# Delta-rule loop: products with keys, decays and head outputs move from GpSimd to VectorE, the squares of keys and queries to ScalarE

## The reference, cut to what matters

```python
q = q / (norm(q) + 1e-06);  k = k / (norm(k) + 1e-06)        # 8 heads of 64
...
def step(carry, ins):                                        # over the 64 tokens
    alpha = sigmoid(at + asp * spike)                        # decay of each channel
    beta  = sigmoid(bt[..., None] + sum(spike * bsp, -1, keepdims=True)) * active
    s = s * alpha[..., None]
    pred = einsum('bhk,bhkv->bhv', kt, s)
    s = s + (beta * kt)[..., None] * (vt - pred)[:, :, None, :]
    out = einsum('bhk,bhkv->bhv', qt, s)
...
y = y * rsqrt(mean(y * y, -1, keepdims=True) + EPS) * head_norm_w
y = x + y.reshape(B, T, H * dv) @ Wo * gate
z = _rms(y, ff_norm_w)
y = y + silu(z @ Wff1) * (z @ Wff3) @ Wff2
```

## Time and profile before

| what | value |
|---|---|
| three timed executions | 2277.12, 2288.8 and 2290.23 us, median 2288.8 |
| profiled execution, span of its instructions | 2277.7 us (its time as a whole is not listed apart from the span) |
| delta stage in it | about 887 to 1854 us of the span |
| busy over the span | PE 80%, DVE 65%, ACT 47%, POOL 32% |
| period of one group in the middle of the loop | 112.7 us: (1708.22 - 1032.03) / 6, from the starts of the first matmul L2341 of groups 1 and 7 |

### The profile page before, as it was taken

How to read it: one execution, slowest core, us unless ns; L and a number is a source line. 1 busy time by engine, 2 the same in 40 slices (tenths; PEclk the granted TensorE clock), 3 DMA queues, 4 the chain that set the end, 5 groups by cost and what they waited for, 6 DMA issues and landing times. The chain is left out here.

```text
span 2277.7 us, 76504 instructions
## 1 busy us (share of the span) xinstructions
PE 1818.4 (80%) x33033; PEld 1305.7 (57%) x33033; DVE 1481.3 (65%) x3245; ACT 1073.9 (47%) x2111; POOL 730.0 (32%) x824
## 2 busy tenths in 40 slices
PE   6999999998688453688989888988886778556774
PEld 4667766766566221365656565656565567544553
DVE  4777777776533776668676868686858343775544
ACT  3666566665233542555555555555554524312322
POOL 0111111111066501435353535353435110306773
PEclk9999999999589786799999999999999965557886
DMA  5000000000211111000000000000000030001114
GB/s 191 12 2 11 11 12 7 2 2 2 88 45 48 45 51 41 7 13 4 17 3 17 3 17 3 17 3 8 8 3 8 3 113 5 11 28 40 53 52 133
DMA packets 43091, 65.02 MB, mean 29 GB/s; under 512 B 6824, under 2 KB 27824, under 8 KB 41992
## 3 DMA queue, kind: packets, MB, share of 16 engines
q1 hardware_dynamic: 35720, 45.70, 6.1%
q0 software_dynamic: 7040, 14.43, 2.2%
HBM read 41.27 MB, written 18.84 MB: 26 GB/s over the span
## 5 line engine op out<-in xcount | busy, mean ns | idle before, releaser
L2800 POOL TENSOR_TENSOR delta_scaled_beta_k<-delta_scaled_beta_k,delta_decays 128x256 f32<-128x256 f32 x160 | 139.4, 893 | 274.3 <-PE bank L2353 274.3
L2920 DVE COPY_PREDICATED delta_neg_a_and_p_t<-delta_level_int,bank 128x512 f32<-128x512 uint8 x192 | 164.2, 923 | 33.5 <-PE bank L2353 24.8
L2353 PE MATMUL bank<-weights_sb,delta_scaled_beta_k 64*64 64x64 f32 x6144 | 121.1, 227 | 74.7 <-POOL delta_scaled_beta_k L2800 44.9
L721 POOL TENSOR_TENSOR attn_probs<-attn_probs,attn_row_sum 128x512 f32<-128x512 f32 x64 | 65.4, 1042 | 344.1 <-DVE attn_row_sum L809 344.1
L2353 PEld LDWEIGHTS bank<-weights_sb,delta_scaled_beta_k 64*64 64x64 f32 x6144 | 108.5, 141 | 96.9 <-issue 96.6
L2957 DVE STREAM_TRANSPOSE delta_inverse_t<-delta_inverse 64x512 f32<-64x512 f32 (+1 forms) x192 | 135.4, 705 | 21.9 <-ACT delta_inverse L2590 20.1
L300 PE MATMUL bank<-attn_z_self_t,weights_sb 128*128 128x256 f32 x512 | 126.4, 386 | 6.7 <-ACT attn_cross_keys L591 3.0
L2584 ACT ACTIVATE delta_two_less_ax<-bank 128x512 f32<-128x512 f32 x160 | 86.5, 597 | 88.0 <-PE bank L2374 86.7
L309 PE MATMUL bank<-attn_w_value_out,attn_z_self_t 128*64 128x512 f32 x512 | 124.3, 606 | 3.0 <-DVE x_all L768 2.7
L617 ACT ACTIVATE attn_probs_t<-bank 128x512 f32<-128x512 f32 x128 | 69.9, 595 | 116.1 <-PE bank L412 116.1
L2590 ACT ACTIVATE delta_inverse<-bank 128x512 f32<-128x512 f32 x128 | 69.3, 595 | 111.3 <-PE bank L2384 111.2
(11 more groups left out here) (545 smaller groups left out, 4665.9 us busy)
## 6 DMA issues: line engine op xcount, KB each, us to landing
weights_sb<-in_w_moe_dram SPq DMA_DIRECT2D x1, 4352.0 KB, 16.8
z_rows<-moe_z_all SPq DMA_DIRECT2D x16, 256.0 KB, 2.6
weights_sb<-moe_outs SPq DMA_DIRECT2D x8, 512.0 KB, 7.3
weights_sb<-in_w_delta_dram SPq DMA_DIRECT2D x1, 2816.0 KB, 11.7
weights_sb<-in_ctx_tok_dram SPq DMA_DIRECT2D x8, 264.0 KB, 4.9
attn_x_channels<-in_x_dram SPq DMA_DIRECT2D x8, 256.0 KB, 3.2
weights_sb<-in_w_self_dram SPq DMA_DIRECT2D x2, 1024.0 KB, 9.2
attn_ctx_channels<-in_ctxT_dram SPq DMA_DIRECT2D x8, 256.0 KB, 2.6
```

The source lines that it names most:

```text
L2353: last = pe.matmul(two[eo][rows(sg), u], kr[r, hp, t], second(kq[r, g % 2, :, hp, t], c), start=first, stop=True, skip_group_check=True)
L2800: pool.tensor_tensor(r_[:, :, 0, :], r_[:, :, 0, :], a_[:, :, 1, 0:1].to_broadcast([128, T // (2 * c), c]), ALU.mult)\
L2920: last = dve.copy_predicated(second(AP[:, eo, hps(P), :, :, :].rearrange("p h b i n -> p (h b i) n"), c), m_, two[eo][:, :].rearrange("p ( ...
```

## The change

Three kinds of products leave GpSimd for VectorE: `scale_k`, `scale_decay` and `o_normed`. On GpSimd the first two were one instruction for each head pair, on VectorE one instruction covers a half, two head pairs, so their counts halve (160 to 80 and 128 to 64); `o_normed` stays at 32. They are put into VectorE's order by hand behind the `scale` of their half, and the head outputs behind the decay products of levels 0 and 1.

The 64 squares of keys and queries leave GpSimd for ScalarE, which now reads bank J twice: first the square, then the copy that frees the bank. The squares of keys still go to `sqk`; those of queries go to the two spaces of `tmp` and the two of `orstd`, which the tail of the group two before uses. So before each square of a query ScalarE waits until the sums of that tail are done (`ss_ps`) and until all its head outputs are normalized (`o_normed`). GpSimd keeps the reset of the mask tile, the token normalization and the residual.

```diff
+
+def q_square(j):
+    return (tmp, orstd)[j // 2][:, j % 2, :]
...
-                last = pe.matmul(out_[r, 0:HALF], cnt_w[:, j, 0:32], sqk[:, j, HALF * half:HALF * half + HALF], start=j == 0,
+                x_ = q_square(j) if q else sqk[:, j, :]
+                last = pe.matmul(out_[r, 0:HALF], cnt_w[:, j, 0:32], x_[:, HALF * half:HALF * half + HALF], start=j == 0,
...
-            pe.wait_ge(s["scaled_kr"], 20 * g + HDP * (l - 1) + 2 * P + 2)
+            pe.wait_ge(s["scaled_kr"], 10 * g + 2 * (l - 1) + P + 1)
...
         for j in js:
             act.wait_ge(s[kind + "_ps"], nth_of(kind, g, j))
+            if kind == "k":
+                if g >= 1:
+                    act.wait_ge(s["nrm_part"], 8 * g)
+                    act.wait_ge(s["q_sum"], g)
+                if g >= 3:
+                    act.wait_ge(s["dn_ps"], g - 2)
+                square_ = sqk[:, j, :]
+            else:
+                if g >= 1:
+                    act.wait_ge(s["nrm_part"], 8 * g)
+                if g >= 2:
+                    act.wait_ge(s["ss_ps"], nth_of("ss", g - 2, 3))
+                    act.wait_ge(s["o_normed"], HDP * (g - 1))
+                square_ = q_square(j)
+            act.activation(square_, J[at_fill[kind, g, j] % 2][:, :], ACT.Square).then_inc(s["squared"], 1)
             act.activation(kq[:, g % 2, 0 if kind == "k" else 1, j, :], J[at_fill[kind, g, j] % 2][:, :], ACT.Copy)\
                 .then_inc(s[kind + "_rd"], 1)
 
...
-    def scale_k(g, l, P):
...
-        for hp in range(2 * P, 2 * P + 2):
...
-            pool.tensor_tensor(r_[:, :, 0, :], r_[:, :, 0, :], a_[:, :, 1, 0:1].to_broadcast([128, T // (2 * c), c]), ALU.mult)\
-                .then_inc(s["scaled_kr"], 1)
...
-    def scale_decay(g, l, P):
...
-    def squares(kind, g):
...
-    def o_normed(g, j):
...
-        if core:
-            scale_k(it, 0, 0)
-        if tail:
-            o_normed(it - 1, 0)
-        if core:
-            scale_k(it, 0, 1)
-        if tail:
-            o_normed(it - 1, 1)
-        if core:
-            scale_decay(it, 0, 0)
-            scale_decay(it, 0, 1)
...
+    def halves(t, c):
+        return t.rearrange("p h (m two c) -> p h m two c", two=2, c=c)
+
+    def scale_k(g, l, P):
+        c = 1 << l
+        dve.wait_ge(s["products"], 14 * g + 2 * (l + 1) + P + 1)
+        if l == 0:
+            dve.wait_ge(s["kr_rd"], nth_of("kr", g, 2 * P + 1))
+        else:
+            dve.wait_ge(s["scaled_kr"], 10 * g + 2 * (l - 1) + P + 1)
+            dve.wait_ge(s["scaled_decay"], 8 * g + 2 * (l - 1) + P + 1)
+        r_, a_ = halves(kr[:, hps(P), :], c), halves(al[:, g % 2, hps(P), :], c)
+        m = T // (2 * c)
+        if c == 1:
+            dve.tensor_tensor(r_[:, :, :, 0, 0], r_[:, :, :, 0, 0], a_[:, :, :, 1, 0], ALU.mult).then_inc(s["scaled_kr"], 1)
+        else:
+            dve.tensor_tensor(r_[:, :, :, 0, :], r_[:, :, :, 0, :], a_[:, :, :, 1, 0:1].to_broadcast([128, 2, m, c]), ALU.mult)\
+                .then_inc(s["scaled_kr"], 1)
+
+    def scale_decay(g, l, P):
+        a_ = halves(al[:, g % 2, hps(P), :], 1 << l)
+        dve.wait_ge(s["scaled_kq"], 24 * g + HDP * (l + 1) + 2 * P + 2)
+        dve.wait_ge(s["scaled_kr"], 10 * g + 2 * l + P + 1)
+        if l > 0:
+            dve.wait_ge(s["scaled_decay"], 8 * g + 2 * (l - 1) + P + 1)
+        dve.tensor_tensor(a_[:, :, :, 0, 0], a_[:, :, :, 0, 0], a_[:, :, :, 1, 0], ALU.mult).then_inc(s["scaled_decay"], 1)
+
+    def o_normed(g, j):
+        dve.wait_ge(s["o_rstd"], HDP * g + j + 1)
+        dve.tensor_tensor(oT[:, j, :], oT[:, j, :], orstd[:, j % 2, :], ALU.mult).then_inc(s["o_normed"], 1)
...
             masked(it, 1, 0)
             scale(it, 0, 0)
             scale(it, 0, 1)
+            scale_k(it, 0, 0)
             masked(it, 1, 1)
             scale(it, 0, 2)
             scale(it, 0, 3)
+            scale_k(it, 0, 1)
+            scale_decay(it, 0, 0)
+            scale_decay(it, 0, 1)
+        if tail:
+            o_normed(it - 1, 0)
+            o_normed(it - 1, 1)
+        if core:
             masked(it, 2, 0)
             scale(it, 1, 0)
             scale(it, 1, 1)
+            scale_k(it, 1, 0)
             masked(it, 2, 1)
             scale(it, 1, 2)
             scale(it, 1, 3)
+            scale_k(it, 1, 1)
+            scale_decay(it, 1, 0)
+            scale_decay(it, 1, 1)
+        if tail:
+            o_normed(it - 1, 2)
+            o_normed(it - 1, 3)
+        if core:
             first_turned(it, 0)
             first_turned(it, 1)
...
             scale(it, 2, 0)
             scale(it, 2, 1)
+            scale_k(it, 2, 0)
             turned(it, 1, 0)
             masked(it, 3, 1)
             scale(it, 2, 2)
             scale(it, 2, 3)
+            scale_k(it, 2, 1)
+            scale_decay(it, 2, 0)
+            scale_decay(it, 2, 1)
             turned(it, 1, 1)
         if front:
```

More of the change, by code:

```diff
@@ L2783, in _ @@
                 def _(pool):
-                    def halves(t, c):
-                        return t.rearrange("p (m two c) -> p m two c", two=2, c=c)
                     def reset(g):
@@ L2852, in _ @@
                         core, front, tail = 0 <= it < NG, 0 <= it + 1 < NG, it >= 1
-                        if core:
-                            scale_k(it, 0, 0)
-                        if tail:
-                            o_normed(it - 1, 0)
-                        if core:
-                            scale_k(it, 0, 1)
-                        if tail:
-                            o_normed(it - 1, 1)
-                        if core:
-                            scale_decay(it, 0, 0)
-                            scale_decay(it, 0, 1)
-                        if tail:
-                            o_normed(it - 1, 2)
-                            o_normed(it - 1, 3)
-                        if core:
-                            scale_k(it, 1, 0)
-                            scale_k(it, 1, 1)
-                            scale_decay(it, 1, 0)
-                            scale_decay(it, 1, 1)
-                        if front:
-                            squares("k", it + 1)
-                        if core:
-                            scale_k(it, 2, 0)
-                            scale_decay(it, 2, 0)
-                            scale_k(it, 2, 1)
-                            scale_decay(it, 2, 1)
-                        if front:
-                            squares("q", it + 1)
-                        if core:
-                            scale_k(it, 3, 0)
-                            scale_decay(it, 3, 0)
-                            scale_k(it, 3, 1)
-                            scale_decay(it, 3, 1)
                         if tail:
                             residual(it - 1)
-                        if core:
-                            scale_k(it, 4, 0)
-                            scale_k(it, 4, 1)
                         if front:
@@ L2935, in scale @@
                         if l > 0:
-                            dve.wait_ge(s["scaled_decay"], 16 * g + HDP * (l - 1) + hp + 1)
+                            dve.wait_ge(s["scaled_decay"], 8 * g + 2 * (l - 1) + hp // 2 + 1)
                         v = kq[:, g % 2, :, hp, :].rearrange("p i (m two c) -> p i m two c", two=2, c=c)[:, :, :, 1, :]
@@ L3103, in _ @@
                             scale(it, 3, 1)
+                            scale_k(it, 3, 0)
                         if front:
@@ L3112, in _ @@
                             scale(it, 3, 3)
+                            scale_k(it, 3, 1)
+                            scale_decay(it, 3, 0)
+                            scale_decay(it, 3, 1)
                             turned(it, 2, 0)
@@ L3120, in _ @@
                             scale(it, 4, 1)
+                            scale_k(it, 4, 0)
                             turned(it, 3, 0)
@@ L3124, in _ @@
                             scale(it, 4, 3)
+                            scale_k(it, 4, 1)
                             turned(it, 3, 1)
```

23 lines of the change are left out of this document (removed).

## The result

| | kernel before | changed kernel |
|---|---|---|
| median of four timed runs | 2288.7 us | 2323.4 us |
| lowest and highest | 2277.1, 2290.2 us | 2320.7, 2326.3 us |
| span of the profiled execution | 2277.7 us | 2324.4 us |

The ratio is 1.0175 [1.0148, 1.0201]: slower by 1.75%, 34.7 us between the medians. The forecast was 2320.

The account below looks back on a forecast made before the run. TensorE leads, with 44.9 us of waits for GpSimd, but VectorE is nearly full; 7.0 us lost less 2.2 gained in each of six groups is 28.8, with the edges +31 on 2288.8: 2320 us, range 2298 to 2340.

Parts of the forecast that it names:

- Steps 1 and 2: First half, group 4: ScalarE's key squares delay the second `first_inverse` to 1395.4; VectorE's last head output follows 6.3 us later.
- Step 3: First half: ScalarE's square of query 0 waits for the last head output, so `f_cb` starts 6.45 us later.
- Step 4: First half: TensorE's clock drops after the idle time; `f_cb` and `t_wo` take 8.4 us, `ax` loses 7.0.
- Second half: The wait before level 4 goes, VectorE is late next; gain 2.2 us per group, ends 0.7 and 4.2.
- about 1 us carried over from level 2: Second half, group 2: delay VectorE was to bring along ahead of its transposes at 1205.16.
- The relief: VectorE gets back about 7 us per group without GpSimd's disturbance, most in `scale`, which would take 0.69 us throughout.
- rival C: Faster: head outputs done before ScalarE asks, at 1395.4, so the new wait is empty; 36 us gained, 2253; chance 0.08.
- Edges: Outside groups 1 to 6: group 0 and stage start 0, group 7 about 3 us longer, last tail 0.7 shorter.
- A: Rival: clock recovers behind the gap and the second half gains more; 0.7 us lost per group, 2295; chance 0.27.
- B: Rival: VectorE limits the second half too, so nothing is gained there; 44 us slower, 2333; chance 0.12.

Follow-up runs that it names:

- run 3: Changed kernel with head outputs 2 and 3 moved ahead of the mask copy of level 1, half 1, in VectorE's queue: 0.9971 of the kernel before.
- run 6: Kernel before with only the squares of keys and queries moved to ScalarE, all products staying on GpSimd: 0.9964 of the kernel before.
- run 8: Kernel before with only key and decay products moved to VectorE, squares and head outputs staying on GpSimd: 1.0114 of the kernel before.
- run 7: Changed kernel with head outputs 2 and 3 ahead of the mask copy and key and decay products back on GpSimd: 0.9915 of the kernel before.
- run 4: Changed kernel with the four head outputs per group back on GpSimd: 0.9986 of the kernel before.
- run 2: Changed kernel with ScalarE copying queries 0 and 1 first and squaring them later from the copies, behind `f_cb`: 1.0093 of the kernel before.
- run 12: Run 7 with only the key squares late, made on ScalarE from the copies behind its part of `f_cb`: 0.9958 of the kernel before.

## Why the prediction was right

**Steps 1 and 2, right.** In group 4, in times of before, the second `first_inverse` ended at 1396.4 (1414.88 + 2.84 - 21.3), forecast 1395.4; ScalarE's queue cost 2.5 us and not 1.5. The last head output ended at 1402.9, forecast 1401.7: 6.5 us behind its releaser where the sum said 6.3.

**Step 3, right.** Six waits of 7.0 to 8.0 us, 45.4 in all. `f_cb` starts 6.3 us later in the mean (26.3 to 32.6), forecast 6.45. Run 3 shows the cause.

**Step 4, right in size.** From `f_cb` to `ax` 8.4 us in the mean, forecast 8.4; it was 7.6. The loss of the first half is 7.2, forecast 7.0. The granted clock of the first half of group 4 was 0.81 where it had been 0.95. But from `f_cb` to `ax` it is only 0.9 us of the loss: before, five of the six `f_cb` (groups 1 to 5) already ran mostly at the low level behind 3.5 us, their first 16 records taking 3.4 to 3.7 us and not 1.95.

**Second half, right, with two terms mis-sized.** Gain 1.8 (78.8 to 77.0), forecast 2.2. The wait before level 4 went, as forecast, since the queries' squares no longer stand ahead of the key product, and VectorE was late next. Counted from `ax`, as means over groups 1 to 6, the products of level 4 start 2.8 us earlier (27.6 to 24.8), the first `xw` behind the wait 1.5 (29.0 to 27.5; in group 2 it waits 2.19 us for VectorE's transposes), the second 2.6 (33.9 to 31.3; forecast 2.1 for group 2). Two terms are off:

- "about 1 us carried over from level 2" did not come. In group 2 the first transposes behind the wait started 0.5 us earlier and not later (1222.67 less 17.97, the distance of the two `ax`, is 1204.70, before 1205.16), and the second ended at 1209.8, forecast 1210.8. The terms as written also give ends 0.5 us later than the 1207.8 and 1210.8 that the sum goes by.
- What comes behind that second `xw` was left out of the sum for groups 1 to 6. From there to the group's end the gain falls from 2.6 to 1.8. VectorE's key products of level 4 lie there, but no run shows that they are the cause.

The runs take the bundle apart. The squares alone give 2.8 in the second half, all of it at that wait (run 6). With the products on VectorE too it is 1.8. In other surroundings the products cost 1.8 (run 8, beside GpSimd's squares) or 2.3 (run 7 against 3, without them), since the transposes stand behind them. The relief itself was as forecast: `scale` of levels 1 to 4 takes 0.68 us in the median and 0.75 at most, where the earlier trace rows had 0.69 and 1.76. Run 6, which has it too, gains nothing beyond that wait, so in the kernel before it was not what the second half stood on.

```profile
L2922 DVE TENSOR_TENSOR weights_sb<-weights_sb,delta_decays x128: 666/683/751, 961.5 to 1820.3; 128x512 f32<-128x512 f32 x128
```

The Trainium skill, "GPSIMD Engine Reference", section "Engine selection", which rival C draws on, has VectorE about twice as fast for a product of two inputs. The trace agrees for one instruction, 0.69 against 1.28 us. As advice it had the wrong sign here: run 4 beats the changed kernel, and run 7 beats run 3, with products on the slower engine. The prediction's other page, "VectorE: DVE Perf Modes" of the Trainium skill, section on the TRN2 errata, also says that its row with 58 cycles is too low for single operations, and gives (N + 151) / 0.96 ns for an f32 addition of two tensors of N elements, 0.69 us for 512; the trace's products agree with that, 0.69 us.

**Edges, too small.** Forecast +2.3 for group 0, group 7 and the last tail together; the profiles have +7.0: group 0 1.4 (99.4 against 98.0), group 7 up to the last token transposes 5.6 (1748.47 to 1881.99, 133.5 against 127.9). In group 7 the wait of 6.02 went as forecast, but `t_wo` now waits 5.4 us there for VectorE's last head output (the longer one of L2299's two waits above), where the sum only let VectorE's queue end 1.3 later. The start of the stage up to group 0 was 2.9 longer, forecast 0. With 32.0 for the six groups (6 x 5.3, forecast 28.8) that is 41.9 of the 46.7 us between the two spans; 4.0 lie ahead of the stage and 0.9 behind it, where nothing was changed. Between the medians there are only 34.7: the profiled execution of before was a short one, near its lowest time, and that of the changed kernel its longest, 2.9 us above the median. So the mechanism was right, but that 31 came so close to 34.7 is partly luck: against the two profiles the sum was a third too small.

**Rivals.** A asked for a clock that stays full behind the gap: it did not, six slow `f_cb` of six. B said that VectorE takes all of the second half's gain: it took 1.0 of 2.8. C decides at 1395.4; run 3 made exactly its condition true, and the loss was gone with it: 0.997 of the kernel before. Its 36 us did not come: of the 6.0 us per group that TensorE had waited for GpSimd, run 3 gained 1.5, since VectorE with the products in its queue was late next.

**Open.** No run separated the longer queue of VectorE from a change in when its operations start, nor was a buffer of their own tried for the query squares. No run on the kernel before kept the squares' place in GpSimd's queue while taking away their disturbance of VectorE.

## What to carry to other kernels

Before moving an operation to the faster engine, follow who waits for its result and what will stand ahead of it in that engine's queue: a product of 1.28 us on an idle engine beat one of 0.69 us behind 5.1 us of other work. A bundle of moves should be priced move by move: here, per group, the squares were worth 1.5 us (2.8 in one half, less 1.3 in the other), the products cost 2.6 to 2.9, and the head outputs cost 7 only by their place. When a part is moved away, look also at what stood behind it in its old queue. Where a copy frees a shared buffer, let nothing with a wait of its own stand ahead of it.

## What the runs showed of the hardware

A GpSimd product slows VectorE's products down, small ones most: beside the squares two decay products of 64 elements took 2.35 us in run 8, alone 0.44 in the changed kernel. Mask copies and transposes kept their length. In group 2 two mask copies took 1.32 us beside the squares before and 1.31 in the changed kernel, where GpSimd stood still, and three transposes took 2.14 beside GpSimd's key products and 2.14 there:

```profile
1201.12 1.32 DVE L2920 COPY_PREDICATED delta_neg_a_and_p_t<-delta_level_int,bank 128x512 f32<-128x512 uint8 x2
1219.30 1.31 DVE L2866 COPY_PREDICATED delta_neg_a_and_p_t<-delta_level_int,bank 128x512 f32<-128x512 uint8 x2
1222.67 2.14 DVE L2934 STREAM_TRANSPOSE delta_inverse_t<-delta_inverse 128x512 f32<-128x512 f32 x3
```

Short idle times of TensorE can weigh more than their length: 3.5 us ahead of `t_wo` cost 1.6 more behind it in five of six groups (run 2). Behind 1.65 us `f_cb` ran fast in group 4 of run 7 and slow in group 4 of run 12, so one such gap alone does not decide it.

When waits for others went, TensorE's gaps without a visible cause grew here: before the products and `xw` they were 35.6 us in the changed kernel (19.6 + 16.0) and 48.7 in run 7, from its waits:

```profile
PE bank L2357 <- issue: 29.8, 28, 2.3
PE bank L2388 <- issue: 18.9, 14, 1.9
```
